# A windowed attention block on one core: the softmax exponent taken in two instructions of 384 columns where there was one of 768

## The chip, the core and the metric

The kernel runs on one core of a Trainium2 chip. The metric is the device time of one execution in microseconds (us), the median of several runs. Five engines run their own instruction streams and meet at semaphores: TensorE (PE, with its weight loads listed apart as PEld), VectorE (DVE), ScalarE (ACT), GpSimd (POOL) and SyncE (SP), which here issues nearly all DMAs.

## What is computed

A shifted-window attention block (4 images, 96 channels, 128 by 128 pixels, 6 heads of 16, windows of 8 by 8 tokens) with its MLP, and after it a divisive normalisation over the channels. Cut to what matters:

```python
y = _ln(x, norm1_w, norm1_b)                       # then rolled by 4 and cut into 8x8 windows
qkv = y @ qkv_w.T + qkv_b
attn = jnp.einsum('bhnd,bhmd->bhnm', q * hd ** (-0.5), k) + mask
attn = jax.nn.softmax(attn, axis=-1)               # over the 64 tokens of a window
out = jnp.einsum('bhnm,bhmd->bnhd', attn, v) @ proj_w.T + proj_b
x = shortcut + out                                 # rolled back
h1 = gelu(_ln(x, norm2_w, norm2_b) @ mlp_w1.T + mlp_b1)
x = x + (h1 @ mlp_w2.T + mlp_b2)
denom_sq = jnp.einsum('nchw,ic->nihw', x * x, gamma_eff) + beta_eff
return x * rsqrt(denom_sq)
```

## The kernel before

The work is cut into 64 units (one row of 16 windows, 1024 tokens) and each unit into two halves of 8 windows, 512 tokens: 128 halves. The loop is a software pipeline over halves. In one round each engine works on several halves at once, at different stages; the constant in each call (`ATTEND`, `MLP`, `SETTLE`, `DIVIDE` and so on) says which half, counted from the current one. Every engine runs a list of steps written out by hand (`steps`, near the end of each engine's block), and that list alone sets its order: an engine never takes a later step while an earlier one waits. Nothing is planned by a scheduler.

Attention, for one half. The 8 windows are 4 pairs; two pairs make a group, so there are two groups (g = 0, 1). For a group:

- TensorE makes the scores (`scores`, L849): 16 matmuls into two PSUM banks, 128 partitions (2 windows of 64 tokens) by 768 columns (2 pairs, 6 heads, 64 keys).
- VectorE takes the row maxima (`max_scores`, L696) and writes scores minus maximum to `shifted` in SBUF (`shift_scores`, L704).
- ScalarE takes the exponent of `shifted` into `probs` (`softmax_exp`, L513), both in SBUF, 768 columns in one instruction.
- TensorE turns `probs` pair by pair, three 128x128 transposes a pair (`turn_probs`, L860) into `probs_t_bank`; ScalarE copies each turn out (`probs_t_copy`, L519). Later come the product with v (`times_v`, L874) and the row sums (`sum_probs`, L884).

Inverses are taken on ScalarE as a logarithm and an exponent, which need one table of functions; the GELU needs another. So each round has two table loads, L558 and L574.

ScalarE's list in one round: table load (L558), first norm's `rstd_of` (L481, L484), `log_sums` (L526), **exponent of group 0** (L513), `log_denominators` (L546), `inverse_sums` (L533), second norm's `rstd_of`, copies of the turned pair 0 and of k, `inverse_denominators`, copy of the turned pair 1, the copies y and q, **exponent of group 1** (L513), table load (L574), GELU 0 (L540), copy of pair 2, GELU 1, GELU 2, copy of pair 3.

TensorE's list in one round: scores of group 0, v (L831), `times_v` and sums of the half before, turn for the second norm (L789), denominators and k (both L803), **turn of pair 0** (L860), `mlp_down` 0 to 2 (nine matmuls, L803), turn of pair 1, turns of the two norms' outputs (L796), scores of group 1, `times_v`, q, projection, turn of x, `mlp_up` 0, **turn of pair 2**, `mlp_up` 1, `mlp_up` 2, turn of pair 3.

Eleven of TensorE's products per round take turns in two PSUM banks, `mm_bank0` and `mm_bank1` (`MM_ITEMS`). A product waits until the one two places ahead of it has been read out. So `mlp_down` 0 waits for `log_den` (the read-out of the denominators), and `mlp_up` 2 waits for GELU 0.

The semaphore `probs_ready` counts exponents: turn of pair p of half A waits for 2A + g + 1, that is, for its whole group.

Of the kernel before, what the change touches and what calls it, by code (L numbers as in the profile page):

```python
# [35 lines left out]
PAIRS = HALF_WINDOWS // 2  # L36
HEAD_PAIRS = HEADS // 2
ROW_TILES = 2
TILE_HEADS = HEADS // ROW_TILES
TILE_DIM = TILE_HEADS * HEAD_DIM  # L40
GROUPS = 2
GROUP_PAIRS = PAIRS // GROUPS
# [14 lines left out]
def window_block(nc, x, qmask, kmask, ident, head_mask, ones_pair, norm1_w, norm1_b, qkv_t, qkv_b,  # L57
# [4 lines left out]
    ACT = mybir.ActivationFunctionType  # L62
# [3 lines left out]
    with ctx:  # L66
        def sb(name, shape, dt=f32):
            return ctx.enter_context(nc.sbuf_tensor(name, shape, dt))
# [4 lines left out]
        def sem(name):  # L73
            return ctx.enter_context(nc.semaphore(name))
# [43 lines left out]
        k = sb("k", [DIM, UNIT])  # L118
# [3 lines left out]
        shifted = sb("shifted", [128, GROUPS, GROUP_PAIRS * TILE_HEADS, ROW_TILES, TOKENS])  # L122
        probs = sb("probs", [128, GROUPS, GROUP_PAIRS, TILE_HEADS, ROW_TILES, TOKENS])
# [60 lines left out]
        probs_ready = sem("probs_ready")  # L184
        probs_turned = sem("probs_turned")
# [48 lines left out]
        def wait(engine, semaphore, count):  # L234

            if not isinstance(count, int) or count > 0:
                engine.wait_ge(semaphore, count)
# [238 lines left out]
        def _(act):  # L476
# [32 lines left out]
            def softmax_exp(A, a, g):  # L509
                group = GROUPS * A + g  # L510
                act.wait_ge(scores_shifted, group + 1)
                wait(act, probs_turned, PAIRS * (A - 1) + GROUP_PAIRS * (g + 1))
                nc.scalar.activation(probs[:, g, :, :, :, :].rearrange("t p j r k -> t (p j r k)"),  # L513
                                     shifted[:, g, :, :, :].rearrange("t i r k -> t (i r k)"), ACT.Exp)\
                    .then_inc(probs_ready, 1)

            def probs_t_copy(A, a, p):
                act.wait_ge(probs_turned, PAIRS * A + p + 1)
# [37 lines left out]
            def steps(run):  # L556

                nc.scalar.preload_act_table_set("natural_log_exp_and_others")  # L558
                run(rstd_of, TURN_OUT, 0)
                run(log_sums, ATTEND - 1)  # L560
                run(softmax_exp, ATTEND, 0)
                run(log_denominators, DIVIDE)
                run(inverse_sums, PROJECT)
                run(rstd_of, MLP, 1)
                run(probs_t_copy, ATTEND, 0)
                run(k_copy, QK)
                run(inverse_denominators, DIVIDE)
                run(probs_t_copy, ATTEND, 1)
                run(y_copy, TURN_OUT, 0)
                run(y_copy, MLP, 1)  # L570

                run(q_copy, QK)
                run(softmax_exp, ATTEND, 1)
                nc.scalar.preload_act_table_set("gelu_and_others")  # L574
                run(gelu, MLP, 0)
                run(probs_t_copy, ATTEND, 2)
                run(gelu, MLP, 1)
                run(gelu, MLP, 2)
                run(probs_t_copy, ATTEND, 3)
# [5 lines left out]
        def _(dve):  # L585
# [105 lines left out]
            def group_scores():  # L691
                return score_banks[:, :, 0:GROUP // ROW_TILES].rearrange("t r (i k) -> t r i k", k=TOKENS)
# [6 lines left out]
            def shift_scores(A, a, g):  # L699

                group = GROUPS * A + g
                dve.wait_ge(max_ready, group + 1)
                wait(dve, probs_ready, group - 1)
                nc.vector.tensor_tensor(shifted[:, g, :, :, :].rearrange("t i r k -> t r i k"), group_scores(),  # L704
                                        row_max[:, g, :, :].unsqueeze(3)
                                        .broadcast_to([128, ROW_TILES, GROUP_PAIRS * TILE_HEADS, TOKENS]),
                                        ALU.subtract).then_inc(scores_shifted, 1)
# [28 lines left out]
            def steps(run):  # L736

                run(max_scores, ATTEND, 0)
                run(v_blocks, ATTEND)
                run(shift_scores, ATTEND, 0)  # L740
                run(statistics, MLP, 1)
                run(normalise, TURN_OUT, 0)
                run(divide, PROJECT)
                run(normalise, MLP, 1)
                run(second_residual, SETTLE)

                run(max_scores, ATTEND, 1)
                run(shift_scores, ATTEND, 1)
                run(split_y2, MLP)
                run(first_residual, PROJECT)  # L750
                run(outputs, DIVIDE)
                run(statistics, TURN_IN, 0)
# [5 lines left out]
        def _(pe):  # L758
# [95 lines left out]

            def turn_probs(A, a, p):
                g, at = p // GROUP_PAIRS, p % GROUP_PAIRS
                pe.wait_ge(probs_ready, GROUPS * A + g + 1)
                wait(pe, probs_t_ready, PAIRS * A + p)
                for m in range(HEAD_PAIRS):
                    made = nc.tensor.transpose(probs_t_bank[:, m * 128:(m + 1) * 128],  # L860
                                               probs[:, g, at, m, :, :], ident_sb[:, :])
                made.then_inc(probs_turned, 1)
# [55 lines left out]
            def steps(run):  # L918

                run(scores, ATTEND, 0)  # L920
                run(project_v, ATTEND)
                run(times_v, ATTEND - 1, 1)
                run(sum_probs, ATTEND - 1)

                run(turn_in, MLP, 1)
                run(denominators, DIVIDE)
                run(project_k, QK)
                run(turn_probs, ATTEND, 0)
                for n in range(HID_CHUNKS):
                    run(mlp_down, SETTLE, n)  # L930
                run(turn_probs, ATTEND, 1)
                run(turn_out, TURN_OUT, 0)
                run(turn_out, MLP, 1)

                run(scores, ATTEND, 1)
                run(times_v, ATTEND, 0)

                run(project_q, QK)
                run(project, PROJECT)
                run(turn_in, TURN_IN, 0)  # L940
                run(mlp_up, MLP, 0)
                run(turn_probs, ATTEND, 2)
                run(mlp_up, MLP, 1)
                run(mlp_up, MLP, 2)
                run(turn_probs, ATTEND, 3)
# [54 lines left out]
```

## Time and profile before

| | |
|---|---|
| time, median of 3 runs | 2130.05 us (2124.49 to 2130.08) |
| the profiled execution | 2125.5 us, of which the span of the instructions 2123.7 us |
| mean granted TensorE clock | 0.994 |
| PE busy | 2015.4 us (95%) |
| PEld busy | 1401.5 us (66%) |
| DVE busy | 1601.8 us (75%) |
| ACT busy | 1645.4 us (77%), 2964 instructions |
| POOL busy | 1611.5 us (76%) |
| exponent L513 | 256 instructions, 845 ns each |

The span runs from the first instruction to the last. The chain of work that ended last is TensorE for 68% of the span, ScalarE for 14% and VectorE for 13%. PE's busy time holds modelled ends of pipelined matmuls, so 95% does not mean that TensorE was never kept waiting. A timeline row gives the start, the time taken and, in brackets, how long the engine had been idle and what ended that. A wait is named after the engine that waited and the instruction that released it.

### The profile page before, as it was taken

The numbers are of one execution on the slowest core, as the hardware profiler recorded it, in microseconds if no ns is written. First come the engines' busy times: TensorE is split into PE (matmuls) and PEld (weight loads), VectorE is DVE, ScalarE is ACT, GpSimd is POOL, SyncE is SP. The second block draws the span as 40 slices with busy tenths as digits, with TensorE's granted clock in tenths as the row PEclk, the third lists the DMA queues.
The fourth block names the chain that finished last, engine by engine and source line by source line (L and its number), as shares of the span: only waits on it lengthen the run. The fifth ranks groups of instructions, "written<-read, shape, count | busy, mean of one in ns | idle before, by whom it ended". The sixth has DMA issues, their size and how long they took to land.

```text
span 2123.7 us, 61985 instructions
## 1 busy us (share of the span) xinstructions
PE 2015.4 (95%) x22532; PEld 1401.5 (66%) x22532; DVE 1601.8 (75%) x4521; ACT 1645.4 (77%) x2964; POOL 1611.5 (76%) x1800
## 2 busy tenths in 40 slices
PE   4899999999999999999999999999999999999996
PEld 2566666666666666666666666666666666666663
DVE  5677777777777777777777777777777777777763
ACT  3787787787787777877877877877877877877876
POOL 2478878878878778878778778778778777877776
PEclk9999999999999999999999999999999999999997
DMA  2112112112212112212212212212212212212110
GB/s 46 32 29 47 39 37 48 38 37 43 44 36 48 39 36 45 42 36 42 45 37 44 42 36 41 46 36 43 44 37 41 46 37 42 45 36 41 38 28 23
DMA packets 217283, 84.49 MB, mean 40 GB/s; under 512 B 117286, under 2 KB 215912, under 8 KB 216984
## 3 DMA queue, kind: packets, MB, share of 16 engines
q1 hardware_dynamic: 216856, 80.33, 19.7%
q8 instruction: 184, 3.01, 0.6%
q14 instruction: 115, 0.94, 0.1%
q0 software_dynamic: 128, 0.20, 0.0%
HBM read 28.03 MB, written 25.17 MB: 25 GB/s over the span
## 4 chain that ended last, share of the span: by engine, by line
PE 68%; ACT 14%; DVE 13%; issue 4%; SPq 1%; POOL 0%; DMA 0%; ACTq 0%; POOLq 0%; DVEq 0%
PE mm_bank L803 28%; PE score_banks L849 10%; PE mm_bank L831 6%; PE probs_t_bank L860 6%; DVE shifted L704 6%; DVE row_max L696 6%; PE turn_bank L796 5%; ACT probs L513 5%; PE mm_bank L884 5%; ACT L574 5%; ACT hidden L540 4%; PE pv_bank L874 3%; PE turn_bank L789 3%; SPq L319 0%; DVE y_tok L669 0%
## 5 line engine op out<-in xcount | busy, mean ns | idle before, releaser
L696 DVE TENSOR_REDUCE row_max<-score_banks 128x12 f32<-128x768 f32 x256 | 245.2, 958 | 408.9 <-PE score_banks L849 408.9
L418 POOL TENSOR_TENSOR hidden_lo<-hidden,hidden_hi 128x512 fp32r<-128x512 f32 x384 | 486.2, 1281 | 0.0
L413 POOL TENSOR_SCALAR attended_hi<-attended 96x512 fp32r<-96x512 f32 x128 | 78.9, 616 | 311.3 <-DVE attended L712 311.3
L669 DVE TENSOR_SCALAR y_tok<-turn_bank,moments,rstd 128x96 f32<-128x96 f32 x1024 | 310.4, 364 | 3.4 <-ACT rstd L484 3.4
L519 ACT ACTIVATE probs_t<-probs_t_bank 128x384 f32<-128x384 f32 x512 | 247.5, 483 | 58.4 <-PE probs_t_bank L860 58.3
L413 POOL TENSOR_SCALAR hidden_hi<-hidden 128x512 fp32r<-128x512 f32 x384 | 237.6, 619 | 45.4 <-ACT hidden L540 39.7
L860 PE MATMUL probs_t_bank<-ident_sb,probs 128*128 128x128 f32 x1536 | 254.2, 274 | 8.5 <-ACT probs_t L519 4.9
L860 PEld LDWEIGHTS probs_t_bank<-ident_sb,probs 128*128 128x128 f32 x1536 | 190.1, 141 | 97.4 <-ACT probs L513 38.0
L540 ACT ACTIVATE hidden<-mm_bank 128x512 f32<-128x512 f32 x384 | 230.4, 600 | 27.6 <-PE mm_bank L803 26.1
L704 DVE TENSOR_TENSOR shifted<-score_banks,row_max 128x768 f32<-128x768 f32 x256 | 245.1, 958 | 8.5
L500 ACT ACTIVATE q<-mm_bank 128x512 f32<-128x512 f32 x128 | 76.5, 598 | 209.4 <-PE mm_bank L803 209.4
L803 PE MATMUL mm_bank<-y_hi,w_hi 97*128 97x512 f32 x384 | 189.5, 493 | 50.2 <-ACT hidden L540 25.9
L513 ACT ACTIVATE probs<-shifted 128x768 f32<-128x768 f32 x256 | 216.4, 845 | 21.2 <-DVE shifted L704 7.5
L849 PE MATMUL score_banks<-k_block,q 64*64 64x192 f32 x4096 | 226.9, 337 | 2.7 <-DMA k_block<-k 2.7
L418 POOL TENSOR_TENSOR y_lo<-y,y_hi 96x512 fp32r<-96x512 f32 x128 | 189.4, 1480 | 23.8 <-POOL y_hi L413 23.8
L658 DVE BATCH_NORM_STATS2 stats<-turn_bank 128x6 f32<-128x96 f32 x1024 | 191.0, 246 | 16.6 <-PE turn_bank L789 16.6
L418 POOL TENSOR_TENSOR x_sq_lo<-x_sq,x_sq_hi 96x512 fp32r<-96x512 f32 x128 | 164.7, 1287 | 23.8 <-POOL x_sq_hi L413 23.8
L418 POOL TENSOR_TENSOR attended_lo<-attended,attended_hi 96x512 fp32r<-96x512 f32 x128 | 162.9, 1272 | 23.8 <-POOL attended_hi L413 23.8
L558 ACT ACT_TABLE_LOAD x138 | 177.1, 1283 | 3.1 <-PEq L988 0.7
L574 ACT ACT_TABLE_LOAD x138 | 177.1, 1283 | 2.4
L803 PE MATMUL mm_bank<-hidden_hi,w_hi 128*96 128x512 f32 x384 | 162.8, 424 | 4.6 <-ACT log_den L546 4.0
L849 PEld LDWEIGHTS score_banks<-k_block,q 64*64 64x64 f32 x4096 | 132.2, 133 | 52.9 <-issue 47.9
(115 smaller groups left out, 4807.6 us busy)
## 6 DMA issues: line engine op xcount, KB each, us to landing
x_ext<-in_x SPq DMA_DIRECT2D x128, 192.0 KB, 3.1
k_block<-k SPq DMA_DIRECT2D x768, 32.0 KB, 2.1
out<-o_ext SPq DMA_DIRECT2D x128, 192.0 KB, 2.6
mask_stage<-in_qmask SPq DMA_DIRECT2D x64, 32.0 KB
y_hi<-mask_stage SPq DMA_DIRECT2D x64, 32.0 KB
k_block<-in_kmask POOLq DMA_DIRECT2D x2, 96.0 KB, 4.6
w_raw<-in_w_t SPq DMA_DIRECT2D x1, 144.0 KB
w<-in_w_t SPq DMA_DIRECT2D x1, 144.0 KB
```

Source lines behind the costliest of these rows:

```text
L413: nc.gpsimd.tensor_scalar(hi, whole, 1.0, 1.0, ALU.mult, ALU.mult).then_inc(hi_ready, 1)
L418: nc.gpsimd.tensor_tensor(lo, whole, hi, ALU.subtract).then_inc(is_split, 1)
L513: nc.scalar.activation(probs[:, g, :, :, :, :].rearrange("t p j r k -> t (p j r k)"), shifted[:, g, :, :, :].rearrange("t i r k -> t (i r ...
L519: nc.scalar.activation(probs_t[:, a % 2, :, p, :], probs_t_bank[:, 0:HEAD_PAIRS * 128] .rearrange("k (p t) -> k p t", p=HEAD_PAIRS), ACT.C ...
L540: nc.scalar.activation(hidden[:, n, :], mm_bank(f"mlp1_{n}", a)[:, :], ACT.Gelu).then_inc(gelu_ready, 1)
L574: nc.scalar.preload_act_table_set("gelu_and_others")
L669: made = nc.vector.tensor_scalar(y_tok[ln][:, c, :], turn_banks[ln][:, n * DIM:(n + 1) * DIM], moments[ln][:, c, 0:1], rstd[ln][:, c:c + 1 ...
L696: nc.vector.tensor_reduce(row_max[:, g, :, :], group_scores(), op=ALU.max, axis=AX.X)\
L704: nc.vector.tensor_tensor(shifted[:, g, :, :, :].rearrange("t i r k -> t r i k"), group_scores(), row_max[:, g, :, :].unsqueeze(3) .broadc ...
L803: made = nc.tensor.matmul(out, w, x_part, start=first and part == 0, stop=last and part == 2)
L849: made = nc.tensor.matmul(score_banks[64 * n:64 * n + 64, r, p * width:(p + 1) * width], q[rows, unit_slot(a), w * TOKENS:(w + 1) * TOKENS ...
L860: made = nc.tensor.transpose(probs_t_bank[:, m * 128:(m + 1) * 128], probs[:, g, at, m, :, :], ident_sb[:, :])
```

## The change

The exponent of a group becomes two instructions, one for each pair, of 384 columns each. The second has its own wait for the buffer `probs`. `probs_ready` now counts pairs, four in a half; `turn_probs` of pair p waits for 4A + p + 1, and VectorE's wait before it overwrites `shifted` counts in pairs for the same event as before.

```diff
             def softmax_exp(A, a, g):
                 group = GROUPS * A + g
                 act.wait_ge(scores_shifted, group + 1)
-                wait(act, probs_turned, PAIRS * (A - 1) + GROUP_PAIRS * (g + 1))
-                nc.scalar.activation(probs[:, g, :, :, :, :].rearrange("t p j r k -> t (p j r k)"),
-                                     shifted[:, g, :, :, :].rearrange("t i r k -> t (i r k)"), ACT.Exp)\
-                    .then_inc(probs_ready, 1)
+                for at in range(GROUP_PAIRS):
+                    wait(act, probs_turned, PAIRS * (A - 1) + GROUP_PAIRS * g + at + 1)
+                    heads = slice(at * TILE_HEADS, (at + 1) * TILE_HEADS)
+                    nc.scalar.activation(probs[:, g, at, :, :, :].rearrange("t j r k -> t (j r k)"),
+                                         shifted[:, g, heads, :, :].rearrange("t i r k -> t (i r k)"),
+                                         ACT.Exp).then_inc(probs_ready, 1)
...
                 dve.wait_ge(max_ready, group + 1)
-                wait(dve, probs_ready, group - 1)
+                wait(dve, probs_ready, GROUP_PAIRS * (group - 1))
...
             def turn_probs(A, a, p):
                 g, at = p // GROUP_PAIRS, p % GROUP_PAIRS
-                pe.wait_ge(probs_ready, GROUPS * A + g + 1)
+                pe.wait_ge(probs_ready, PAIRS * A + p + 1)
                 wait(pe, probs_t_ready, PAIRS * A + p)
```

ScalarE's order, place one, in a round in the middle of the program: from the logarithm of the row sums to the next inverse. Names are output<-inputs; in brackets the semaphores waited for. Before:

```order
L526 ACTIVATE log_sum<-mm_bank 96x512 [waits sums_made]
L513 ACTIVATE probs<-shifted 128x768 [waits probs_turned,scores_shifted]
L546 ACTIVATE log_den<-mm_bank 96x512 [waits inv_den_ready,den_made]
L533 ACTIVATE inv_sum<-log_sum 96x512 [waits attended_ready,log_sum_made]
L481 ACTIVATE log_var<-moments,eps_col 128x4 [waits moments_ready2]
```

and after the change, two source lines lower from the exponent on:

```order
L528 ACTIVATE log_sum<-mm_bank 96x512 [waits sums_made]
L515 ACTIVATE probs<-shifted 128x384 [waits probs_turned,scores_shifted]
L515 ACTIVATE probs<-shifted 128x384 [waits probs_turned]
L548 ACTIVATE log_den<-mm_bank 96x512 [waits inv_den_ready,den_made]
L535 ACTIVATE inv_sum<-log_sum 96x512 [waits attended_ready,log_sum_made]
L481 ACTIVATE log_var<-moments,eps_col 128x4 [waits moments_ready2]
```

Nothing else has moved: `log_den` stands behind two instructions in place of one.

ScalarE's order, place two, the later part of a round, from the copy of q to the first GELU (`hidden`) and the copy of pair 2. Before:

```order
L500 ACTIVATE q<-mm_bank 128x512 [waits q_made]
L513 ACTIVATE probs<-shifted 128x768 [waits probs_turned,scores_shifted]
L574 ACT_TABLE_LOAD
L540 ACTIVATE hidden<-mm_bank 128x512 [waits mlp1_made,hidden_split]
L519 ACTIVATE probs_t<-probs_t_bank 128x3x128 [waits probs_turned]
```

and after:

```order
L500 ACTIVATE q<-mm_bank 128x512 [waits q_made]
L515 ACTIVATE probs<-shifted 128x384 [waits probs_turned,scores_shifted]
L515 ACTIVATE probs<-shifted 128x384 [waits probs_turned]
L576 ACT_TABLE_LOAD
L542 ACTIVATE hidden<-mm_bank 128x512 [waits mlp1_made,hidden_split]
L521 ACTIVATE probs_t<-probs_t_bank 128x3x128 [waits probs_turned]
```

Here the table load and the first GELU stand behind the two. TensorE's instructions and their order are as they were.

## Rows read from the trace of the kernel before

**Rows 1.** The page, busy time of each engine.

```profile
PE 2015.4 (95%) x22532; PEld 1401.5 (66%) x22532; DVE 1601.8 (75%) x4521; ACT 1645.4 (77%) x2964; POOL 1611.5 (76%) x1800
```

**Rows 2.** Waits: engine, line, releaser: us in total, times, longest.

```profile
DVE row_max L696 <- PE score_banks L849: 408.9, 256, 4.6
...
PEld mm_bank L803 <- ACT hidden L540: 81.0, 128, 0.6
...
PEld probs_t_bank L860 <- ACT probs L513: 38.0, 130, 2.3
...
PEld mm_bank L803 <- ACT log_den L546: 26.3, 127, 2.2
```

**Rows 3.** Timeline around group 0's exponent: start, us taken, engine, instruction, [idle before].

```profile
999.53 0.85 ACT L513 ACTIVATE probs<-shifted 128x768 f32<-128x768 f32 x1
...
1014.49 0.96 DVE L704 TENSOR_TENSOR shifted<-score_banks,row_max 128x768 f32<-128x768 f32 x1
...
1015.48 0.85 ACT L513 ACTIVATE probs<-shifted 128x768 f32<-128x768 f32 x1
...
1016.19 0.39 PE L803 MATMUL mm_bank<-y_lo,wk_hi 97*96 97x512 f32 x1
1016.23 0.58 ACT L546 ACTIVATE log_den<-mm_bank 96x512 f32<-96x512 f32 x1
...
1016.38 0.31 PEld L860 LDWEIGHTS probs_t_bank<-ident_sb,probs 128*128 128x128 f32 x3 [0.27 <-ACT probs L513]
1016.42 0.52 PE L860 MATMUL probs_t_bank<-ident_sb,probs 128*128 128x128 f32 x3
...
1016.86 0.16 PEld L803 LDWEIGHTS mm_bank<-hidden_hi,w_hi 128*96 128x96 f32 x1 [0.17 <-ACT log_den L546]
```

**Rows 4.** Timeline around group 1's exponent, the round before.

```profile
1006.32 0.96 DVE L704 TENSOR_TENSOR shifted<-score_banks,row_max 128x768 f32<-128x768 f32 x1
...
1007.31 0.84 ACT L513 ACTIVATE probs<-shifted 128x768 f32<-128x768 f32 x1
...
1008.17 1.28 ACT L574 ACT_TABLE_LOAD   x1
...
1009.47 0.60 ACT L540 ACTIVATE hidden<-mm_bank 128x512 f32<-128x512 f32 x1
...
1010.12 0.19 PEld L803 LDWEIGHTS mm_bank<-y_hi,w_hi 97*128 97x128 f32 x1 [0.64 <-ACT hidden L540]
```

**Rows 5.** Timeline from group 0's turn on to the scores of group 1.

```profile
1018.28 1.22 DVE L669 TENSOR_SCALAR y_tok<-turn_bank,moments,rstd 128x96 f32<-128x96 f32 x4
...
1018.80 0.48 PEld L860 LDWEIGHTS probs_t_bank<-ident_sb,probs 128*128 128x128 f32 x3
1019.03 0.49 PE L860 MATMUL probs_t_bank<-ident_sb,probs 128*128 128x128 f32 x3
...
1019.36 1.04 PE L796 MATMUL turn_bank<-ident_sb,y_tok 128*96 128x128 f32 x8
...
1020.33 0.88 PE L849 MATMUL score_banks<-k_block,q 64*64 64x192 f32 x16
```

**Rows 6.** Groups by line and shape: count | busy us, mean ns | idle before.

```profile
L519 ACT ACTIVATE probs_t<-probs_t_bank 128x384 f32<-128x384 f32 x512 | 247.5, 483 | 58.4 <-PE probs_t_bank L860 58.3
...
L513 ACT ACTIVATE probs<-shifted 128x768 f32<-128x768 f32 x256 | 216.4, 845 | 21.2 <-DVE shifted L704 7.5
...
L533 ACT ACTIVATE inv_sum<-log_sum 96x512 f32<-96x512 f32 x128 | 79.1, 618 | 0.0
...
L484 ACT ACTIVATE rstd<-log_var 128x4 f32<-128x4 f32 x256 | 52.7, 206 | 8.1
```

**Rows 7.** Timeline of ScalarE, three instructions that follow one another.

```profile
1017.55 0.20 ACT L484 ACTIVATE rstd<-log_var 128x4 f32<-128x4 f32 x1
...
1017.66 0.48 ACT L519 ACTIVATE probs_t<-probs_t_bank 128x384 f32<-128x384 f32 x1
...
1018.03 0.58 ACT L506 ACTIVATE k<-mm_bank 96x512 f32<-96x512 f32 x1
```

## The prediction, made before the changed kernel ran

> **What bounds the kernel now.** I read the busy shares first. TensorE is busy for 95% of the span and no other engine for more than 77% [rows 1]. By that alone a change on ScalarE would be free. The reader should distrust this, because busy matmuls have modelled ends and the share is an average over a whole round. So I read the waits next. TensorE's weight loads wait in every one of the 128 rounds for two read-outs by ScalarE: for the first GELU (81.0 us, 128 times) and for the logarithm of the denominators (26.3 us, 127 times) [rows 2]. They also wait 130 times for the exponent itself, 38.0 us in all [rows 2]. VectorE in turn waits for the scores 256 times, that is for both groups of every round [rows 2]. So work passes back and forth between engines, and I followed it in the timeline.
>
> A round takes 1015.48 - 999.53 = 15.95 us, from one exponent of group 0 to the next [rows 3]. The loop closes like this. Group 0: VectorE's shift ends at 1015.45, the exponent starts 0.03 later and ends at 1016.33, `log_den` starts behind it at 1016.23 and ends at 1016.81, and 0.05 later, at 1016.86, TensorE gets its bank for `mlp_down` [rows 3]. From there TensorE runs without a listed wait for 3.47 us to the scores of group 1 at 1020.33 [rows 5]. Group 1 (read one round earlier): the shift ends at 1007.28, the exponent starts at 1007.31 and ends at 1008.15, the table load takes 1008.17 to 1009.45, the first GELU 1009.47 to 1010.07, and TensorE gets the bank for `mlp_up` 2 at 1010.12 [rows 4]. Then it runs on to the next scores of group 0, for which VectorE waits, and the loop is closed. The exponent stands in this loop twice, both times with gaps of a few hundredths on either side. That is what bounds the kernel: a ring of latencies, two exponents of it on ScalarE.
>
> **What the change removes.** TensorE's turn of pair 0 need not wait for the second half of the exponent. Its probabilities come about 0.85 - 0.52 = 0.33 us earlier (0.52 is derived below). What is that worth? In the trace the weight loads of this turn had been idle 0.27 us when they started at 1016.38, but its first matmul started at 1016.42, and the last matmul of k, the step ahead of it, at 1016.19 [rows 3]. That is 0.23 us of distance, no more than TensorE's own pace: the nine matmuls of 512 columns of `mlp_down` stand between 1016.86 and 1019.03 [rows 3, 5], 0.24 us each. So at most some hundredths are to be had, and even these go nowhere: the next step, `mlp_down`, starts at 1016.86 only because `log_den` ended at 1016.81 [rows 3]. Whatever the turn gains, it waits there. The gain is zero. For the turns of pairs 1, 2 and 3 no wait for an exponent recurs: pair 1 is turned at 1019.03, 2.7 us after the exponent's end [rows 3, 5], and the count of 130 waits for 128 rounds [rows 2] leaves room for one a round, which is pair 0's.
>
> The Trainium skill speaks for a gain here. Its page "TensorE: Matmul & The Clock Gate", section "Step-by-step: what each phase is for", says that weight loads are pulled ahead of matmuls still in flight. The trace agrees: pair 1's loads start at 1018.80 and its matmuls at 1019.03 [rows 5], so pair 0's loads would move up by about as much. By the rule alone TensorE would win up to the 38.0 us that these loads waited; by the row on `log_den` nothing. I take nothing, and keep the other as a rival.
>
> **What it adds.** One more ScalarE instruction per group, 256 in all. Price of one exponent of 384 columns, SBUF to SBUF: the exponent of 4 columns takes 206 ns and that of 768 takes 845 [rows 6]. The line through them has (845 - 206) / 764 = 0.836 ns a column and gives 206 + 380 x 0.836 = 524 ns. Neighbours overlap: the 768-column exponent takes 0.85 us but `log_den` starts 0.75 after it [rows 3]; the 4-column one takes 0.20 and the next starts after 0.11, a 384-column copy takes 0.48 and the next starts after 0.37 [rows 7]. So about 0.10 us of overlap. Two exponents then last 2 x 524 - 100 = 948 ns in place of 845: **0.10 us more per group**. `log_den` starts later by the same, since it would start 2 x 0.424 = 0.85 after the first exponent instead of 0.75.
>
> Bounds of that price. From below: the 384-column copy, which reads PSUM, takes 483 ns and lets the next start after 0.37 [rows 6, 7]. By it the pair costs 2 x 0.37 - 0.75 = -0.01 us for `log_den`, and 2 x 483 - 100 - 845 = +21 ns to the end. In between: the line from 512 columns (618 ns) to 768 (845) [rows 6] gives 505 ns for 384, so +65 ns. From above: if the second exponent began only when the first had ended, 2 x 524 - 845 = +203 ns. I take 0.10, because the two rows nearest in kind (the same function, both SBUF to SBUF, both on 128 partitions) give it; the 512-column row is on 96 partitions and the copy reads elsewhere.
>
> The Trainium skill has a price too. The page "ScalarE: Activation LUTs", section "What ACT_TABLE_LOAD costs", gives an instruction without pointer operands as 186 ns plus 0.833 ns a column and an overlap of about 93 ns between neighbours. By that one more instruction costs 186 - 93 = 93 ns, an estimate of 24 us over 256 of them and a time of 2149 us; the PSUM copy of 483 ns speaks for a cheaper one, since the page's figure for 384 columns would be 506.
>
> **How much of it reaches the end.** Group 0: `log_den` ends 0.10 later, so `mlp_down` starts 0.10 later, since nothing else held it (it followed `log_den` by 0.05). Do the 3.47 us behind it swallow that? They are TensorE's own run. The one thing it could have been waiting for, VectorE's `y_tok`, is ready at 1019.50, while the four matmuls that read it are the last of eight between 1019.36 and 1020.33, so from about 1019.85 [rows 5]: TensorE was the later one by 0.35 and stays so. The scores of group 1 come 0.10 later, and with them VectorE's maximum and shift. Group 1: exponents, table load, GELU 0 and `mlp_up` 2 follow without slack, TensorE having been idle before it (0.64 us for the weight load [rows 4]). Another 0.10. The next scores of group 0 are 0.20 late. Nothing has slack across the whole ring, so the loss adds up in every round.
>
> Sum: 128 rounds x 2 x 0.10 = 25.6 us. Other parts cost nothing: the second wait for `probs_turned` is for turns of the half before, long past, and rides on its instruction; behind the second exponent of group 0 also stand the inverse of the sums, the second norm's `rstd` and the copies, but their users are kept later by VectorE and TensorE themselves (see `y_tok` above), and this cover would be gone only at a delay over 0.35; the wait of VectorE on `shifted` is for the same event.
>
> The sum is made against the profiled execution, 2125.5 us (span 2123.7 and 1.8 around it), which lies 4.6 under the median of the three runs and 1.0 above the fastest. 2125.5 + 25.6 = **2151 us**.
>
> **The rivals.**
> - *The wait that goes was real* (the other side). If TensorE did lose the time that its loads waited for the exponent, and if `log_den` came early enough in most rounds, 38.0 us would come back: 2087; with the 25.6 paid besides, 2113. It decides for faster from the point at which the turn of pair 0, and not `log_den`, is the last thing before `mlp_down`. For it: 130 waits. Against it: 127 waits for `log_den` in the same rounds, and the matmul distance of 0.23.
> - *Two halves are as cheap as the whole.* ScalarE takes both at the copy's price: -0.01 to +0.02 per group, -3 to +5 us, 2123 to 2131. For it: the 0.37 us distance. Against it: exponents from SBUF have higher rows at every size.
> - *No overlap between the two exponents*, for instance because the second holds a wait of its own: 256 x 0.203 = 52 us, 2177. For it: nothing in the trace; `log_den` has two waits and still starts 0.10 before the exponent ends, which speaks against.
>
> **How the numbers follow.** Forecast 0.83, with a price between 0.055 and 0.14 us, 2140 to 2161; gain 0.03; halves as cheap as the whole 0.07; no overlap 0.07. The range 2140 to 2163 takes the forecast's own, and 2 us upward because the runs' median lay above the profiled one. About 0.3% (6.4 us) is what a measurement of this kernel can tell from no change; that is a price of 0.025 per group. Faster 0.03, same 0.07, slower 0.90.
>
> **What the changed profile would show.** Exponents of 384 columns, 512 of them, near 524 ns, the second starting 0.42 after the first, and `log_den` 0.85 after the first. The weight loads of pair 0's turn no longer wait for an exponent, but those of `mlp_down` wait longer for `log_den` (26.3 us would grow to 26.3 plus about 13 and what the turn gained), and those of `mlp_up` 2 for GELU 0 by 13 us (81.0 to 94). The round is 16.15 us. I am wrong if the round is 15.95 or less, if the 384-column exponents take under 490 ns or over 560, or if the loss appears at one of the two places only.

## The result, and the profile after

The changed kernel takes 2152.92 us (median of 4 runs, 2148.19 to 2153.75) against 2127.27 us for the kernel before on the same chip (its three runs above and a fourth, 2123.56): a ratio of 1.0117, 95% interval 1.0103 to 1.0130. It is slower, by 25.7 us, where 25.6 and a time of 2151 were forecast. The profiled executions are 2125.5 us before and 2148.2 after, both at a mean granted TensorE clock of 0.994.

The page of the changed kernel, to be read beside [rows 1]. TensorE's busy share falls while the kernel gets slower, and ScalarE's work grows by 24 us in 256 more instructions:

```profile
PE 2019.7 (94%) x22532; PEld 1408.6 (66%) x22532; DVE 1600.7 (75%) x4521; ACT 1669.2 (78%) x3220; POOL 1620.2 (75%) x1800
```

Its waits, beside [rows 2] (us in total, times, longest):

```profile
DVE row_max L698 <- PE score_banks L851: 433.4, 256, 4.0
...
PEld mm_bank L805 <- ACT hidden L542: 94.3, 128, 1.1
...
PEld mm_bank L805 <- ACT log_den L548: 40.3, 127, 2.1
...
PEld probs_t_bank L862 <- ACT probs L515: 5.1, 5, 2.2
```

The two waits of TensorE's loads for ScalarE's read-outs grew: for GELU 0 from 81.0 to 94.3, for `log_den` from 26.3 to 40.3. VectorE waits 24.5 us longer for the scores, 408.9 to 433.4: that is the whole loss, seen from the engine that stands between the two groups.

The exponent's own line in the changed kernel (count, shortest, median and longest in ns, and who waited for it):

```profile
L515 ACT ACTIVATE probs<-shifted x512: 506/514/527, 46.6 to 2099.1; 128x384 f32<-128x384 f32 x171
...
  PEld probs_t_bank L862: 9.0, 7
  PE probs_t_bank L862: 2.6, 2
```

Before, the loads of the turn waited 130 times for the exponent, 38.0 us [rows 2]. Now they wait 7 times, 9.0 us (the list of waits above books five of the seven, 5.1 us, under the exponent), and none of these lies between 120 and 2060 us. The wait that the change removes is gone, and nothing was gained by it. The timeline around group 0's exponent, beside [rows 3], shows why:

```profile
1010.10 0.96 DVE L706 TENSOR_TENSOR shifted<-score_banks,row_max 128x768 f32<-128x768 f32 x1
...
1011.10 0.94 ACT L515 ACTIVATE probs<-shifted 128x384 f32<-128x384 f32 x2
...
1011.81 0.39 PE L805 MATMUL mm_bank<-y_lo,wk_hi 97*96 97x512 f32 x1
1011.81 0.48 PEld L862 LDWEIGHTS probs_t_bank<-ident_sb,probs 128*128 128x128 f32 x3
...
1011.94 0.58 ACT L548 ACTIVATE log_den<-mm_bank 96x512 f32<-96x512 f32 x1
1012.04 0.49 PE L862 MATMUL probs_t_bank<-ident_sb,probs 128*128 128x128 f32 x3
...
1012.57 0.16 PEld L805 LDWEIGHTS mm_bank<-hidden_hi,w_hi 128*96 128x96 f32 x1 [0.28 <-ACT log_den L548]
```

The loads of the turn now start 0.23 ahead of its matmuls. The matmuls themselves start 1.94 after the shift's start, and before it was 1016.42 - 1014.49 = 1.93 [rows 3]. The two exponents take 0.94 in place of 0.85, `log_den` starts 1.84 after the shift instead of 1.74, and `mlp_down` 2.47 instead of 2.37. So `mlp_down` is 0.10 us late behind group 0. The same around group 1, beside [rows 4]:

```profile
1017.97 0.96 DVE L706 TENSOR_TENSOR shifted<-score_banks,row_max 128x768 f32<-128x768 f32 x1
...
1018.96 0.94 ACT L515 ACTIVATE probs<-shifted 128x384 f32<-128x384 f32 x2
...
1019.92 1.28 ACT L576 ACT_TABLE_LOAD   x1
...
1021.22 0.60 ACT L542 ACTIVATE hidden<-mm_bank 128x512 f32<-128x512 f32 x1
...
1021.86 0.19 PEld L805 LDWEIGHTS mm_bank<-y_hi,w_hi 97*128 97x128 f32 x1 [0.74 <-ACT hidden L542]
...
1026.25 0.96 DVE L706 TENSOR_TENSOR shifted<-score_banks,row_max 128x768 f32<-128x768 f32 x1
```

From the shift's start to the load for `mlp_up` 2 it is 3.89 us; before it was 1010.12 - 1006.32 = 3.80 [rows 4]. The table load follows at 1.95 and not at 1.85. The round is 1026.25 - 1010.10 = 16.15 here and 16.134 in the median of all the rounds of the trace, against 15.946 in the same median of before: 0.188 a round, 24.1 us over 128.

### The profile page after: what moved, and what is told of

It is laid out like the page before. It is cut to its first block, busy times and chain, and to the rows that moved or that the text cites. A ratio compares the mean times of both kernels' runs of the same rounds, so it can differ in the third digit from the quotient of the medians.

```text
span 2146.4 us, 62241 instructions
## 1 busy us (share of the span) xinstructions
PE 2019.7 (94%) x22532; PEld 1408.6 (66%) x22532; DVE 1600.7 (75%) x4521; ACT 1669.2 (78%) x3220; POOL 1620.2 (75%) x1800
## 4 chain that ended last, share of the span: by engine, by line
PE 55%; DVE 18%; ACT 16%; issue 10%; SPq 1%; POOL 0%; DMA 0%; ACTq 0%; POOLq 0%; DVEq 0%
PE mm_bank L805 23%; PE score_banks L851 10%; DVE shifted L706 9%; PE mm_bank L833 6%; ACT probs L515 6%; DVE row_max L698 6%; PE turn_bank L798 5%; PE probs_t_bank L862 5%; ACT L576 4%; ACT hidden L542 4%; PE mm_bank L886 2%; DVE v_block L687 2%; ACT log_den L548 2%; PE pv_bank L876 2%; PE turn_bank L791 1%
## 5 line engine op out<-in xcount | busy, mean ns | idle before, releaser
L698 DVE TENSOR_REDUCE row_max<-score_banks 128x12 f32<-128x768 f32 x256 | 245.1, 957 | 433.4 <-PE score_banks L851 433.4
L515 ACT ACTIVATE probs<-shifted 128x384 f32<-128x384 f32 x512 | 240.6, 517 | 21.5 <-DVE shifted L706 7.5
L862 PEld LDWEIGHTS probs_t_bank<-ident_sb,probs 128*128 128x128 f32 x1536 | 199.7, 141 | 85.0 <-issue 6.2
L542 ACT ACTIVATE hidden<-mm_bank 128x512 f32<-128x512 f32 x384 | 230.4, 600 | 26.1 <-PE mm_bank L805 24.5
L418 POOL TENSOR_TENSOR y_lo<-y,y_hi 96x512 fp32r<-96x512 f32 x128 | 197.6, 1544 | 23.8 <-POOL y_hi L413 23.8
```

The lines of the kernel that those rows point to most:

```text
L418: nc.gpsimd.tensor_tensor(lo, whole, hi, ALU.subtract).then_inc(is_split, 1)
L515: nc.scalar.activation(probs[:, g, at, :, :, :].rearrange("t j r k -> t (j r k)"), shifted[:, g, heads, :, :].rearrange("t i r k -> t (i r ...
L542: nc.scalar.activation(hidden[:, n, :], mm_bank(f"mlp1_{n}", a)[:, :], ACT.Gelu).then_inc(gelu_ready, 1)
L698: nc.vector.tensor_reduce(row_max[:, g, :, :], group_scores(), op=ALU.max, axis=AX.X)\
```

## The experiments

In all of them "a round" is the median distance between two group 0 shifts in the kernel's own trace (15.946 in the kernel before), and the ratio is to the kernel before, run on the same chip. In the diffs `...` marks lines left out.

**One group alone in two instructions.** The other keeps its whole exponent. Edit, shown for the whole one:

```diff
+                if g != 0:                      # second kernel: g != 1
+                    wait(act, probs_turned, PAIRS * (A - 1) + GROUP_PAIRS * (g + 1))
+                    nc.scalar.activation(<all 768 columns>, ACT.Exp).then_inc(probs_ready, GROUP_PAIRS)
+                    return
```

> Only the exponent of group 0 is taken in two instructions; group 1 keeps one of 768 columns. My theory (a ring of latencies that holds both exponents; one more instruction costs 0.095 us wherever it stands in the ring): half of the change's loss, 128 x 0.095 = 12 us, ratio to before about 1.006, a round of 16.04 us, log_den 0.095 later, GELU 0 unmoved against the scores. Rival (only the table load or the GELU behind group 1's exponent feels it): 0 us, ratio 1.000. Rival (only log_den feels it): 24 us, ratio 1.012.

Measured: 2145.02 us, ratio 1.0082 (1.0068 to 1.0096), a round of 16.090.

> Only the exponent of group 1 is taken in two instructions; group 0 keeps one of 768 columns. My theory: the other half, 12 us, ratio about 1.006, a round of 16.04 us, GELU 0 0.095 later after the scores of group 1. Rival (only the table load or the GELU feels it): 24 us, ratio 1.012. Rival (only log_den feels it): 0 us, ratio 1.000.

Measured: 2147.97 us, ratio 1.0088 (1.0076 to 1.0101), a round of 16.093. Both rivals fell, since either group costs something; but so did my number. Each half of the change cost 0.145 a round, and together they would make 0.29 where the whole change makes 0.188. The traces named a suspect. The exponent that was left whole began 0.05 us later after VectorE's shift than in the kernel before, and both its waits stood in an instruction of their own. What my edit had added to it was the step of 2 on `probs_ready`. The next three runs test this.

**The same with steps of 1** (three exponents in a half, and the counts waited for to match):

```diff
-                    ACT.Exp).then_inc(probs_ready, GROUP_PAIRS)
+                    ACT.Exp).then_inc(probs_ready, 1)
...
-                pe.wait_ge(probs_ready, PAIRS * A + p + 1)
+                pe.wait_ge(probs_ready, 3 * A + (1, 2, 3, 3)[p])      # group 1 alone: (1, 1, 2, 3)
```

> As the earlier run with group 0 alone in two instructions, but every exponent, whole or half, raises probs_ready by 1 (three in a half), as the kernel before did; there the whole exponent of group 1 raised it by 2, and in its trace that instruction began 0.05 us later after VectorE's shift than before, with both waits in an instruction of their own. My theory (0.095 us for the added instruction, 0.05 for the step of 2): a round of 16.04 us where it was 16.09, ratio to before about 1.006. Rival (half the split costs more than half because the ring is not additive): 16.09 us and 1.008 again.

Measured: 2136.49 us, ratio 1.0046 (1.0033 to 1.0058), a round of 16.038.

> The same for group 1 alone: every exponent raises probs_ready by 1. My theory: a round of 16.04 us, ratio about 1.006; the whole exponent of group 0 starts 0.03 after the shift's end again. Rival (not additive): 16.09 us and 1.009 again.

Measured: 2140.93 us, ratio 1.0062 (1.0048 to 1.0075), a round of 16.044. The rounds are 0.092 and 0.098 over before, and their sum, 0.190, is that of the whole change, 0.188. By the rounds the ring is additive. The medians of the times say the same more roughly: 9.4 and 13.9 us over the kernel before on that chip, 23.3 together. In the waits each loss stands where it was put. Group 0 alone:

```profile
PEld mm_bank L812 <- ACT hidden L548: 82.0, 128, 1.0
...
PEld mm_bank L812 <- ACT log_den L554: 39.0, 127, 2.1
```

Group 1 alone:

```profile
PEld mm_bank L812 <- ACT hidden L548: 93.6, 128, 1.1
...
PEld mm_bank L812 <- ACT log_den L554: 26.2, 127, 2.1
```

**The step of 2 by itself**, in the kernel before (the count that VectorE waits for is doubled too):

```diff
-                    .then_inc(probs_ready, 1)
+                    .then_inc(probs_ready, 2)
...
-                pe.wait_ge(probs_ready, GROUPS * A + g + 1)
+                pe.wait_ge(probs_ready, 2 * (GROUPS * A + g + 1))
```

> The kernel before, unchanged but for the step by which an exponent raises probs_ready: 2 instead of 1, with the counts waited for doubled. Nothing is split or moved. My theory (the step of 2 takes the waits off the instruction and puts them into one of their own, and the exponent begins 0.05 us later): two exponents a round, a round of 16.05 us instead of 15.95, ratio to before about 1.006. Rival (the 0.05 came from something else in those kernels): a round of 15.95 us, ratio 1.000.

Measured: 2138.70 us, ratio 1.0054 (1.0040 to 1.0068), a round of 16.053, so 0.107 for two exponents. The shift and ScalarE in its timeline:

```profile
1006.37 0.96 DVE L704 TENSOR_TENSOR shifted<-score_banks,row_max 128x768 f32<-128x768 f32 x1
...
1007.41 0.85 ACT L513 ACTIVATE probs<-shifted 128x768 f32<-128x768 f32 x1 [0.15 <-DVE shifted L704]
1008.16 0.58 ACT L546 ACTIVATE log_den<-mm_bank 96x512 f32<-96x512 f32 x1
```

The instruction takes as long as ever and starts 1.04 after the shift's start instead of 0.99. Half of the 0.107 is 0.054 for one exponent, and the excess of the first two runs, which had one each, was 0.052 (16.090 - 16.038) and 0.049 (16.093 - 16.044). So the excess was the edit's own.

**Four instructions of 192 columns per group.** The changed kernel, each half cut once more, only the last of each pair of instructions raising the semaphore:

```diff
+                    for c in range(2):
+                        cols = slice(192 * c, 192 * (c + 1))
+                        made = nc.scalar.activation(dst[:, cols], src[:, cols], ACT.Exp)
+                    made.then_inc(probs_ready, 1)
```

> Four exponents of 192 columns per group instead of two of 384, with the changed kernel's waits. My theory (a fixed price per instruction, columns cost the same however they are cut): three more instructions than before per group, 3 x 0.095 x 256 = 73 us, ratio about 1.034, a round of 16.52 us; a 192-column exponent takes about 0.365 us and the next starts 0.27 after it. Rival (the price is that of the second wait, not of the instruction): the two added here have no wait, so as the changed kernel, 1.012. Rival (slack in the ring takes up only small delays or bounds them): not in proportion; below 1.025.

Measured: 2197.32 us, ratio 1.0327 (1.0312 to 1.0343), a round of 16.504. That is 0.558 over before for six added instructions, 0.093 each, the same as for the two of the change, 0.094 each. The four that were added to the changed kernel cost 16.504 - 16.134 = 0.370, 0.093 each. A piece of 192 columns takes 352 ns, where 365 was said. The group's line and its place in the timeline:

```profile
L519 ACT ACTIVATE probs<-shifted 128x192 f32<-128x192 f32 x1024 | 288.0, 352 | 21.3 <-DVE shifted L709 7.4
```

```profile
999.85 1.13 ACT L519 ACTIVATE probs<-shifted 128x192 f32<-128x192 f32 x4
1000.88 0.57 ACT L551 ACTIVATE log_den<-mm_bank 96x512 f32<-96x512 f32 x1
```

768 columns take 0.85, 0.94 and 1.13 us in one, two and four pieces. The price belongs to the instruction, and not to the second wait, which the added ones do not have.

**The finer wait alone.** The changed kernel, but each turn waits for both pairs of its group:

```diff
-                pe.wait_ge(probs_ready, PAIRS * A + p + 1)
+                pe.wait_ge(probs_ready, PAIRS * A + GROUP_PAIRS * (g + 1))
```

> The changed kernel, but each turn waits for both pairs of its group, as before the change. My theory (the finer wait is worth nothing, since mlp_down waits for log_den anyway): as the changed kernel, 1.011 to 1.012 over before, a round of 16.13 us; the turn of pair 0 starts 0.05 later than in the changed kernel and mlp_down at the same place. Rival (the finer wait gives time back and the two instructions cost more than the result shows): slower than the changed kernel by up to 38 us, 1.02 to 1.03.

Measured: 2152.64 us, ratio 1.0115 (1.0102 to 1.0128), a round of 16.134, to the nanosecond that of the changed kernel. The long waits of the loads moved from the row of `log_den` back to that of the exponent:

```profile
PEld probs_t_bank L862 <- ACT probs L515: 50.7, 131, 2.7
...
PEld mm_bank L805 <- ACT log_den L548: 26.5, 127, 2.1
```

The loads wait 45.6 us more for the exponents (50.7 against 5.1 in the same list) and 13.8 less for `log_den` (26.5 against 40.3), 32 us more in all, and the kernel is as fast. So the idle time of the loads is no measure of what can be won. The matmuls tell it: in the median of all rounds the first one of pair 0's turn starts 1.99 after the shift instead of 1.93, and `mlp_down` at 2.46 in both kernels. The wait by pair is worth nothing as long as `log_den` stands behind both halves.

**log_den between the halves.** If that is the reason, the split can be made to pay: group 0 in two instructions with `log_denominators` run between them, group 1 whole, steps of 1 and the counts as in the run with group 0 alone.

```diff
-                run(softmax_exp, ATTEND, 0)
+                run(exp_pair, ATTEND, 0, 0)
                 run(log_denominators, DIVIDE)
+                run(exp_pair, ATTEND, 0, 1)
```

> Group 0 in two instructions with log_den run between them, group 1 whole, steps of 1. My theory (mlp_down waits for log_den alone, and the turn of pair 0 needs only the first half of the exponent): log_den ends about 2.00 after the shift's start instead of 2.32 (2.41 in the changed kernel), mlp_down starts at about 2.26, right behind the turn, instead of 2.37; round 15.84 us, 0.11 under before, 14 us in all, ratio to before 0.993 to 0.995. The second half of the exponent, done by 2.45, is not needed before 4.5. Rival (what counts is ScalarE's total, as it has one more instruction): slower than before by 12 us, 1.006. Rival (the turn of pair 0 or inv_sum's users become the last): 1.000.

Measured: **2106.34 us** (2101.43 to 2107.82), ratio 0.9895 (0.9879 to 0.9912), a round of 15.756. It beats both kernels, by 21 us and by 47. The gain over before is 0.190 a round and not the 0.11 that I had worked out. The timeline:

```profile
1007.64 0.96 DVE L713 TENSOR_TENSOR shifted<-score_banks,row_max 128x768 f32<-128x768 f32 x1
...
1008.63 0.53 ACT L521 ACTIVATE probs<-shifted 128x384 f32<-128x384 f32 x1
...
1009.08 0.60 ACT L554 ACTIVATE log_den<-mm_bank 96x512 f32<-96x512 f32 x1
...
1009.57 0.51 ACT L521 ACTIVATE probs<-shifted 128x384 f32<-128x384 f32 x1
1009.58 0.49 PE L869 MATMUL probs_t_bank<-ident_sb,probs 128*128 128x128 f32 x3
...
1009.80 0.16 PEld L812 LDWEIGHTS mm_bank<-hidden_hi,w_hi 128*96 128x96 f32 x1
1009.82 0.47 PE L812 MATMUL mm_bank<-hidden_hi,w_hi 128*96 128x512 f32 x1
```

`log_den` ends at 1009.68, 2.04 after the shift's start, and `mlp_down` starts with no wait, 2.18 after it, 0.24 behind the start of the turn. I had allowed 0.32 for the three transposes; in the median of this trace the third starts 0.22 after the first, and `mlp_down` 0.03 after that. The trace of the kernel before had it already, behind the turn of pair 2, where the next product starts 1008.98 - 1008.73 = 0.25 after the turn:

```profile
1008.73 0.49 PE L860 MATMUL probs_t_bank<-ident_sb,probs 128*128 128x128 f32 x3
...
1008.98 0.47 PE L803 MATMUL mm_bank<-y_hi,w_hi 97*128 97x512 f32 x1
```

The turn of pair 0 itself starts 1.94 after the shift in both kernels (median). So from here on `mlp_down` follows TensorE's own work and no longer ScalarE's. In the waits of this kernel `log_den` has nearly vanished, with 5.6 us where before had 26.3:

```profile
PEld mm_bank L812 <- ACT log_den L554: 5.6, 4, 2.2
```

**The same with group 1 in two as well**, so the changed kernel with `log_den` one place up:

```diff
-                run(softmax_exp, ATTEND, 1)
+                run(exp_pair, ATTEND, 1, 0)
+                run(exp_pair, ATTEND, 1, 1)
```

> As the run with log_den between the halves, and group 1 in two instructions as well: the changed kernel with log_den moved one place up. My theory: 0.095 us a round above it: 15.93 us, ratio to before 0.999 to 1.000, so the move gives back what the split cost, 0.20 us a round against the changed kernel. Rival (ScalarE's total counts): as the changed kernel, 1.012.

Measured: 2117.18 us, ratio 0.9956 (0.9943 to 0.9968), a round of 15.850. Group 1's split costs 0.094 again (15.850 - 15.756); the move of one line is worth 0.284 against the changed kernel. The expected ratio, 0.999 to 1.000, stood on the 0.11 of the run before and missed with it.

**Is the split needed for that?** The kernel before, whole exponents, `log_den` ahead of group 0's:

```diff
-                run(softmax_exp, ATTEND, 0)
                 run(log_denominators, DIVIDE)
+                run(softmax_exp, ATTEND, 0)
```

> The kernel before with whole exponents, and log_den moved ahead of the exponent of group 0. Theory (the gain of the version with log_den between the halves needs the split, because log_den can't start before its product is there, 1.43 us after the shift's start, and the exponent is ready at 0.99): the exponent runs 1.92 to 2.77, the turn of pair 0 follows it, mlp_down starts at about 3.07 instead of 2.37; 0.70 a round, 90 us, ratio 1.042. Rival (the order alone brings the gain, the split nothing): 0.989 or lower.

Measured: 2222.38 us, ratio 1.0447 (1.0431 to 1.0464), a round of 16.701.

```profile
1009.82 0.96 DVE L704 TENSOR_TENSOR shifted<-score_banks,row_max 128x768 f32<-128x768 f32 x1
...
1011.26 0.59 ACT L546 ACTIVATE log_den<-mm_bank 96x512 f32<-96x512 f32 x1 [0.56 <-PE mm_bank L803]
...
1011.75 0.83 ACT L513 ACTIVATE probs<-shifted 128x768 f32<-128x768 f32 x1
...
1012.63 0.31 PEld L860 LDWEIGHTS probs_t_bank<-ident_sb,probs 128*128 128x128 f32 x3 [1.18 <-ACT probs L513]
```

ScalarE idles 0.56 us for the product that `log_den` reads, and the turn then waits for the exponent. The order alone loses 96 us, 0.755 a round where 0.70 was expected; in the median of the rounds `mlp_down` starts 3.12 after the shift, where 3.07 was expected. So the split is needed: the half exponent fills the time until `log_den` can start. The wait by pair should be needed there too. With `log_den` between the halves the second half ends 2.44 after the shift (1010.08 - 1007.64), so a turn that waited for it would start about 0.5 us later than it does. That is an estimate from the timeline above; no run has `log_den` between the halves and the coarse wait.

## Why the prediction was right

- *What bounds the kernel.* The ring of latencies with both exponents in it is shown by the single splits: 0.092 and 0.098 us a round, alone, and 0.188 together, each in its own row of the waits. TensorE's busy share (95%) would have said that ScalarE costs nothing.
- *What the change removes.* Forecast at nothing. The loads' wait for the exponent did go (38.0 to 5.1 us in the lists of waits), the loads moved up ahead of the matmuls (1011.81 and 1012.04), and the run with the coarse wait put back has the same round. The first rival, a gain, needed `log_den` to be out of the way. In the kernel where it is, the gain is 0.190 a round, with the price of the split paid.
- *What it adds.* Forecast 0.10 us a group from the line through the exponents of 4 and 768 columns; measured 0.094, and 0.093 in the run with four pieces. The two exponents take 517 ns in the mean where 524 was forecast; in the median the first takes 525 and the second, which starts 0.43 after it, 509. The lower bounds, from the PSUM copy and from the 512-column row, were both too cheap. The estimate of 93 ns for one more instruction, worked out from the figures of the Trainium skill (page "ScalarE: Activation LUTs", section "What ACT_TABLE_LOAD costs"), agrees with the 94 ns measured here.
- *How much reaches the end.* All of it, as forecast: 24.1 us by the rounds, 22.7 between the profiled executions, 25.7 between the medians (2152.92 and 2127.27), for 25.6 in the sum. That the difference of the medians meets the sum to a tenth is luck: by the rounds, taken inside one trace of each kernel, each group costs 0.094 and not 0.10. The round came to 16.13 where 16.15 was said, the wait for GELU 0 to 94.3 where 94 was said, that for `log_den` to 40.3.
- *The rival without overlap* fell: `log_den` starts 1.84 after the shift, not 1.94.

What I had wrong lies in the expectations behind it: that a step of 2 on a semaphore is free, and that the turn's three transposes hold TensorE for 0.32 us before the next matmul may start, which sized two runs wrongly (15.84 for 15.756 and 15.93 for 15.850).

## What to carry to other kernels

A wait in the profile is worth only what the next wait on the same engine leaves of it; look for the one that stands behind it before making it finer, and on TensorE look at when the matmuls start, not at how long the loads were idle. Cutting an instruction that lies in a ring of latencies costs its fixed price each time round (here 0.094 us for one more, with ScalarE busy for 77% of the span); it paid here when what TensorE waits for next was run between the pieces. An experiment's edit can cost something itself: when two parts add up to more than the whole, look for what the edit added.

## What the runs showed of the hardware that I had not expected

An exponent that raises its semaphore by 2 does not carry its wait. In the kernel before only the wait for the buffer `probs` stands in an instruction of its own, an EVENT_SEMAPHORE of 17 ns, and the exponent itself carries the wait for the shift. With the step of 2 both waits stand ahead in one EVENT_SEMAPHORE, and the exponent began 0.05 us later after VectorE's shift (1.04 against 0.99 us). With two such in a round it cost 0.107 us a round and 0.54% of the kernel's time. Only exponents on ScalarE were tried. Whether the chip or the way the program is built asks for this is open; no run tells them apart.
